# Four bias tables for three and six score buffers for four in a fused four-layer kernel

## Time and profile before

| | |
|---|---|
| median of 3 runs | 2759.53 us (2757.42 to 2760.26) |
| the profiled execution | 2763.53 us |
| its span in the profile | 2762.2 us |
| TensorE's mean granted clock in the span | 0.984 of full speed |
| instructions | 62626 |
| issues of `ld_bt` | 256, 512 KB each, 3.9 us to landing |

### The profile page before, as it was taken

The page is one execution under the profiler, slowest core; times in us unless marked ns, Lnnn a source line. Parts: engine busy times, 40 slices in busy tenths (PEclk is TensorE's granted clock), DMA queues, the critical chain, the costliest instruction groups (busy, mean ns, idle before and its releaser), DMA issues.

```text
span 2762.2 us, 62626 instructions
## 1 busy us (share of the span) xinstructions
PE 2615.9 (95%) x20072; PEld 2223.2 (80%) x20072; DVE 2240.4 (81%) x7925; ACT 2343.2 (85%) x5285; POOL 1696.2 (61%) x1742
## 2 busy tenths in 40 slices
PE   8878999999999999999999999999999999999998
PEld 7767788888888888888888888888888888888776
DVE  5668888888888888898888888888888888888763
ACT  1667899999889899888989888889898898998875
POOL 3666676666667666666666566666666666656431
PEclk8999999999999999999999999999999999999998
DMA  6433334333333333333333333333333333333211
GB/s 228 132 97 100 93 111 118 113 95 104 110 99 106 115 116 91 103 105 103 113 113 100 104 109 93 105 115 114 91 103 107 98 115 111 100 101 102 76 29 30
DMA packets 176405, 287.96 MB, mean 104 GB/s; under 512 B 45840, under 2 KB 99088, under 8 KB 175696
## 3 DMA queue, kind: packets, MB, share of 16 engines
q1 hardware_dynamic: 176080, 283.97, 34.9%
HBM read 174.64 MB, written 8.45 MB: 66 GB/s over the span
## 4 chain that ended last, share of the span: by engine, by line
PE 73%; ACT 10%; SPq 6%; issue 4%; DVE 3%; DMA 2%; POOL 2%; ACTq 0%; DVEq 0%; POOLq 0%
PE bank L1181 15%; PE bank L1174 15%; PE bank L1202 11%; PE bank L1159 10%; PE bank L1151 8%; PE bank L1194 5%; SPq L415 4%; PE bank L1166 3%; ACT PB L993 2%; DMA Ks<-KU 2%; PE bank L1220 2%; ACT BB L1014 2%; SPq L411 2%; PE bank L1309 2%; PE bank L1221 2%
## 5 line engine op out<-in xcount | busy, mean ns | idle before, releaser
L993 ACT ACTIVATE PB<-PB,mx 128x256 f32<-128x256 f32 (+1 forms) x2048 | 841.0, 475 | 10.1 <-DVE mx L789 9.1
L797 DVE TENSOR_TENSOR PO<-bank,PH 128x384 f16<-128x384 f32 (+1 forms) x1024 | 589.8, 617 | 153.7 <-ACT PH L999 149.7
L500 POOL TENSOR_TENSOR BT<-BT,MN 128x1024 f32<-128x1024 f32 x256 | 546.9, 2137 | 116.5 <-DMA BT<-in_bias 115.6
L999 ACT ACTIVATE PH<-bank 128x384 f16<-128x384 f32 (+1 forms) x1024 | 502.7, 540 | 100.2 <-PE bank L1202 99.0
L1194 PE MATMUL bank<-Ks,Qs 96*128 96x512 f32 (+1 forms) x1024 | 521.3, 513 | 62.5 <-DVE mx L789 33.7
L1202 PE MATMUL bank<-ident,PB 128*128 128x128 f32 x3584 | 495.1, 277 | 20.9 <-DVE PO L797 14.0
L789 DVE CUSTOM_DVE_ANT_0 PB<-bank,BT 128x256 f32<-128x256 f32 x1024 | 389.4, 418 | 112.3 <-issue 81.8
L1202 PEld LDWEIGHTS bank<-ident,PB 128*128 128x128 f32 x3584 | 419.4, 143 | 68.0 <-ACT PB L993 32.2
L789 DVE CUSTOM_DVE_ANT_0 PB<-bank,caus 128x128 f32<-128x128 f32 (+1 forms) x1024 | 321.5, 352 | 55.6 <-PE bank L1194 34.5
L1220 PEld LDWEIGHTS bank<-VP,PH 128*128 128x128 f16 x3584 | 204.8, 96 | 112.8 <-issue 104.1
L1194 PEld LDWEIGHTS bank<-Ks,Qs 96*128 96x128 f32 x1024 | 195.1, 191 | 91.8 <-DVE mx L789 38.6
(11 more groups left out here) (225 smaller groups left out, 5247.0 us busy)
## 6 DMA issues: line engine op xcount, KB each, us to landing
BT<-in_bias SPq DMA_DIRECT2D x256, 512.0 KB, 3.9
Qs<-QH SPq DMA_DIRECT2D x512, 64.0 KB, 2.5
Ks<-KH SPq DMA_DIRECT2D x1024, 32.0 KB, 2.0
Qs<-QU SPq DMA_DIRECT2D x256, 64.0 KB, 2.7
Ks<-KU SPq DMA_DIRECT2D x512, 32.0 KB, 2.0
XT<-in_xT SPq DMA_DIRECT2D x32, 256.0 KB, 4.4
X<-in_x SPq DMA_DIRECT2D x32, 256.0 KB, 2.9
AB<-ada_rows SPq DMA_DIRECT2D x32, 256.0 KB, 3.4
```

The lines of the kernel that those rows point to most:

```text
L500: G.op.tensor_tensor(v2(BT[k % 3]), v2(BT[k % 3]), MN[:, :].unsqueeze(1).broadcast_to([128, 2, 512]), ALU.add).then_inc(g_bt, 1)
L797: V.op.tensor_tensor(PO[i][:, 0:w], bP[h][:, 0:w], PH[i][:, 0:w], ALU.subtract).then_inc(v_low, 1)
L993: S.op.activation(o, o, ACT.Exp, scale=-1.0, bias=mx[u.layer][:, c:c + 1]).then_inc(a_exp, 1)
L999: S.op.activation(PH[i][:, 0:w], bP[h][:, 0:w], ACT.Copy).then_inc(a_high, 1)
```

## The change

The bias tables `BT` become four in place of three: table k goes to `BT[k % 4]`, its load waits for unit k-4 of layer 1 in place of k-3, and there is a fourth semaphore. The score buffers `PB` become six in place of four: unit D uses `PB[(2 * D + q) % 6]`, and its bias waits for the transposes of unit D-3 in place of D-2. To make room, `Gm` keeps its first half only; the second half is loaded by a transfer of its own into the sixth score buffer before any score needs it. `ti` and `fold` move into the fifth score buffer. All places stay as they are.

```diff
-        fold = sb("fold", [128, 2])
-        Gm = sb("Gm", [128, 1024])
+        Gm = sb("Gm", [128, 512])
...
-        BT = [sb(f"BT{i}", [128, 1024]) for i in range(3)]
+        BT = [sb(f"BT{i}", [128, 1024]) for i in range(4)]
...
-        PB = units_of("PB", 4)
+        PB = units_of("PB", 6)
...
-        ti = sb("ti", [128, 32], I32)
...
-        z0, z1, z2, z3 = PB
+        z0, z1, z2, z3, z4, z5 = PB
+        ti = z4[:, 0:32].bitcast(I32)
+        fold = z4[:, 32:34]
...
-                        if k >= 3:
-                            S.wait_ge(v_bias, bias_of(number[1, (k - 3) // 8, (k - 3) % 8], 1, 1))
-                        S.op.dma_start(BT[k % 3][:, :], A["bias"][u.b, u.n]).then_inc(d_bt[k % 3], 16)
+                        if k >= 4:
+                            S.wait_ge(v_bias, bias_of(number[1, (k - 4) // 8, (k - 4) % 8], 1, 1))
+                        S.op.dma_start(BT[k % 4][:, :], A["bias"][u.b, u.n]).then_inc(d_bt[k % 4], 16)
...
-                        S.op.dma_start(Gm[:, :], A["G"]).then_inc(d_G, 16)
+                        S.op.dma_start(Gm[:, :], A["G"][:, 0:512]).then_inc(d_G, 16)
+                        S.op.dma_start(z5[:, :], A["G"][:, 512:1024]).then_inc(d_G, 16)
...
-                        G.wait_ge(d_bt[k % 3], 16 * (k // 3 + 1))
+                        G.wait_ge(d_bt[k % 4], 16 * (k // 4 + 1))
                         G.wait_ge(g_mn, u.b + 1)
-                        G.op.tensor_tensor(v2(BT[k % 3]), v2(BT[k % 3]), MN[:, :].unsqueeze(1).broadcast_to([128, 2, 512]),
+                        G.op.tensor_tensor(v2(BT[k % 4]), v2(BT[k % 4]), MN[:, :].unsqueeze(1).broadcast_to([128, 2, 512]),
...
-                blk = [Gm[:, 128 * i:128 * i + 128] for i in range(8)]
-                V.wait_ge(d_G, 16)
+                blk = [w[:, 128 * i:128 * i + 128] for w in (Gm, z5) for i in range(4)]
+                V.wait_ge(d_G, 32)
...
                         V.wait_ge(p_score, score_of(D, q))
-                        V.wait_ge(p_flip, head_of(D - 2, 1))
+                        V.wait_ge(p_flip, head_of(D - 3, 1))
...
-                            V.op.tensor_tensor_reduce(PB[(2 * D + q) % 4][:, h * 256:h * 256 + w], bS[q][:, h * w:h * w + w],
+                            V.op.tensor_tensor_reduce(PB[(2 * D + q) % 6][:, h * 256:h * 256 + w], bS[q][:, h * w:h * w + w],
...
-                            c, o = 4 * u.n + 2 * q + h, PB[(2 * u.D + q) % 4][:, h * 256:h * 256 + w]
+                            c, o = 4 * u.n + 2 * q + h, PB[(2 * u.D + q) % 6][:, h * 256:h * 256 + w]
...
-                                                  PB[(2 * u.D + q) % 4][:, h * 256 + k * 128:h * 256 + k * 128 + 128], ident[:, :])
+                                                  PB[(2 * u.D + q) % 6][:, h * 256 + k * 128:h * 256 + k * 128 + 128], ident[:, :])
```

More of the change, by code:

```diff
@@ L243, in build @@
         d_x, d_xn, d_ab = sems("d_x d_xn d_ab")
-        d_m, d_bt, d_st, d_out = sems("d_m0 d_m1"), sems("d_bt0 d_bt1 d_bt2"), sems("d_st0 d_st1"), sems("d_out0 d_out1")
+        d_m, d_bt, d_st, d_out = sems("d_m0 d_m1"), sems("d_bt0 d_bt1 d_bt2 d_bt3"), sems("d_st0 d_st1"), sems("d_out0 d_out1")
         g_const, g_zero, v_set, a_set, p_set, v_cf, v_mv = sems("g_const g_zero v_set a_set p_set v_cf v_mv")
@@ L358, in loads @@
             conditioning(d_wc0, 0, 1)
-            S.op.dma_start(ti[:, :], A["itok"].unsqueeze(0).broadcast_to([128, 32])).then_inc(d_it, 16)
+            S.op.dma_start(ti, A["itok"].unsqueeze(0).broadcast_to([128, 32])).then_inc(d_it, 16)
             conditioning(d_wc1, 1, 5)
@@ L599, in vector @@
             V.wait_ge(d_it, 16)
-            V.op.tensor_copy(tv[:, 2, :], ti[:, :]).then_inc(v_set, 1)
+            V.op.tensor_copy(tv[:, 2, :], ti).then_inc(v_set, 1)
             V.wait_ge(v_set, 12)
@@ L785, in attention @@
                             if x == 1:
-                                plus = BT[k % 3][:, h * 512 + q * 256:h * 512 + q * 256 + 256]
+                                plus = BT[k % 4][:, h * 512 + q * 256:h * 512 + q * 256 + 256]
                             else:
                                 plus = caus[:, 128:256] if q == 0 else caus[:, :]
-                            V.op.tensor_tensor_reduce(PB[(2 * D + q) % 4][:, h * 256:h * 256 + w], bS[q][:, h * w:h * w + w],
+                            V.op.tensor_tensor_reduce(PB[(2 * D + q) % 6][:, h * 256:h * 256 + w], bS[q][:, h * w:h * w + w],
                                                       plus, -1.0, 3.0e38, ALU.add, ALU.min,
```

## The result

The kernel after takes 2774.2 us (median of 5 runs, 2769.7 to 2775.8), the kernel before in the same job 2759.5 (5 runs, 2757.4 to 2762.6). The ratio is 1.0046, 95% interval 1.0035 to 1.0058: **slower by 0.5%**, where 0.7% faster was forecast. The profiled execution of after took 2773.3 us, with a span of 2772.0 against 2762.2. Most lines of after are one higher than before: L1195 is L1194, L790 is L789, L893 is L892, L501 is L500. In the kernels of the experiments they stand a few lines further down.

What follows compares the result with a forecast made beforehand. TensorE, busy 95%, was taken as the bound, so only its waits counted. Savings of 18.2 and 1.4 make 19.6, taking the profiled 2763.5 to 2743.9; the median, 4.0 lower, gives 2740 us, range 2728 to 2758.

Steps and rivals of the forecast that it cites:

- B goes wholly: TensorE's wait for the `Ks` copy before the score matmul (L1194) vanishes between 320 and 2576 us: minus 18.2 us.
- 80.24 plus its B: Batch length in us: 80.24 plus TensorE's full wait for the `Ks` copy, with nothing behind that wait catching it up.
- Start of the kernel: Between 100 and 320 us the `Ks` copy waits shrink: 0 to minus 2.8 us, taken as minus 1.4.
- first A: A is TensorE's wait before the score matmul for VectorE's row maximum, 33.7 us in total, forecast to stay unchanged.
- Six score buffers at 0: Bias waiting for unit D-3's transposes removes VectorE idles but gains TensorE 0; bound 0 to 33.7 us.
- The cover of 0.5: Six buffers were to prevent a new 0.5 us TensorE wait before unit 7's transposes; bound 5.5 us if it arises.
- the rival that it goes: The 0.5 us wait before unit 7's transposes arises, or the row-maximum wait grows: 2745 to 2758 us, chance 0.09.
- Earlier loads meet the copies of units 4 and 5 on the way ... I take 0: Bias-table loads issued earlier share the way with query and key copies, without delaying their landing: cost 0.
- cover gone: Rival: new 0.5 us wait before unit 7's transposes, or a longer row-maximum wait; 2745 to 2758 us, chance 0.09.
- the second rival: Low TensorE clocks in series: alike batches each fall to 0.98, adding 1.7 us each, up to 2776; chance 0.20.
- The rival's price of 1.7 each: In the low-clocks-in-series rival, each batch at mean clock 0.98 adds 1.7 us over 80.24.

Runs made afterwards that it cites:

- the best version: The changed kernel (four tables, six score buffers) with unit 7's GpSimd mask addition waiting until VectorE has done both pairs and the subtraction between: 2743.7 us, ratio 0.9940.
- the extra addition: Three tables and six score buffers, plus one GpSimd addition per batch to a table nothing reads, directly behind unit 6's mask addition: 2815.5 us, ratio 1.0200.

## Why the prediction was wrong

**B goes wholly: right.** No wait on `Ks<-KU` is left between 320 and 2576 us. Its worth was a little over-sized. Without B and without the hold a batch is 80.39, not 80.24: with B of 0.33 to 0.35 a batch of before was 80.56 to 80.60, so only 0.2 of such a B comes back. "80.24 plus its B" was read from batches that all had a B, and it doesn't hold down to none. Of the batch from 1108.66 in before and the one from 1267.52 with the addition moved, the latter has the score 0.59 earlier, and the matmuls at L1177 only 0.33 earlier at +6.01. Over 27 batches this is 4 us. What catches up the rest, these runs don't show.

**Start of the kernel: smaller.** The first A of the steady stretch ends 0.65 earlier than before (379.27 against 379.92), where 1.4 was taken.

**Six score buffers at 0: right** for the kernel with three tables and for the batch at full clock; with the hold away the medians are 0.9940 and 0.9955 of before with and without them, which the intervals don't tell apart. They did remove VectorE's unnamed idle of the earlier trace rows (0.2 us is left at L790), as forecast. The cover of 0.5, and the rival that it goes, were both empty.

**The step that failed** is the one on the earlier loads: "Earlier loads meet the copies of units 4 and 5 on the way ... I take 0". It priced an earlier load as a transfer alone, and as a transfer it was right: by the medians no copy takes longer to land. What I weighed there was only whether transfers share their engines. The load is also what GpSimd waited for at L500 (1.65 to 4.06 in the batches of before), and a load that lands earlier lets that addition start earlier. Which instructions of VectorE then lie under it was never asked. What the runs showed in its place is the pair at 2.17 for 0.24, and 1.16 more per batch at full clock, against some 0.5 (14.1 over 27 batches) that B gave back. I named the place of a new wait (before the transposes, from late low parts) only as "cover gone".

**The clock: half right.** Nine batches of after, eight of them in a row, have a mean clock of 0.98, against six before: the series that the second rival feared from batches that are all alike. But it is not the main part of the loss, since the batches at full clock carry the hold. In the kernels without B a low-clock batch takes 81.9 to 82.1, whether the batch at full clock is 80.4, 80.6 or 81.55, so one costs 1.55 in the best version and 0.4 in after. In such a batch the hold adds nothing that can be seen: 81.92 to 82.01 with it in after, 81.94 to 82.03 in the three such batches of the best version that have no hold. The rival's price of 1.7 each is what such a batch has over 80.24; no kernel had batches of 80.24. The number of low-clock batches differs from execution to execution, and whether the hold or the missing B has a part in it, these runs don't show.

**The account** for the 27 batches from the first A to the last (379.27 to 2585.09 in after, 2205.8; before 379.92 to 2575.65, 2195.7): 27 times 80.39 is 2170.5. The 18 batches of after at full clock have 21.3 more than that, which is the hold; the nine low-clock batches have 14.0 more, which is the clock. (With all 27 at full clock the hold would be 27 times 1.16, or 31.3; so its share is between 21 and 31, by which of the two is counted first.) The same for the best version: 2170.5, four low-clock batches, 6.3, and 0.2 for the rest, against a measured 2177.0. Against before that is 18.8 less: the 18.2 of B, less the 4.1 that doesn't come back, and 4.8 because the low clocks cost 11.1 before (2195.7 less 27 times 80.24 and less 18.2; the hold of the batch of 82.63 is in it) and 6.3 here, less the 0.2. After against before is 10.1 more: 21.3 for the hold and 2.9 for the low clocks, less the 14.1 of B. The term that the prediction lacked took 21.3 in this execution, more than all that it had added up.

## What to carry to other kernels

When a change makes a buffer free or a load land earlier, follow the data one step further: which instruction waited for that load, on which engine, and what does it fall on now? If that engine is GpSimd, list VectorE's instructions with two SBUF inputs in the new place, and count GpSimd's unbroken run, not one instruction. A wait that keeps GpSimd's work where it was can turn such a loss into the gain that was meant: 1.0046 became 0.9940 here by one condition and one wait. And look at busy times, not only at waits: the held pair shows as a longer instruction (844 ns on average in place of 181) and stands in no table of waits.

## What the runs showed of the hardware

- A 128 x 8 VectorE operation with both inputs in SBUF (two in 0.24 us) took 2.17 us under a GpSimd addition of 2.13, and 2.26 under two of 1.15 back to back. It did not get in between them in 14 of 16 batches; in two it did, after 1.21. Under three additions of 2.13 in a row it took 4.2. Where GpSimd's run ended and a gap of 0.34 us followed (the extra addition), it went through.
- The hold is not the pair's alone: `AA<-AA` (128 x 508, two SBUF inputs) took 2.43 to 2.65 in place of 0.68 where it was the one to meet the addition.
- In the same places VectorE's instructions with one SBUF input kept their times: `BATCH_NORM_STATS2` 0.69 and the bias (PSUM and SBUF) 0.42.
- The other direction is there too: GpSimd's addition of 2.13 took 2.54 where it started at +8.74 while VectorE ran `AA<-AA` (two SBUF inputs, +8.61, 0.68).
- A batch with a mean granted clock of 0.98 took 81.9 to 82.1 in all seven kernels without B, while the batch at full clock ranged from 80.39 to 81.63.
